# Four of eight contraction tiles of a fused adapter chain computed as a seven-product block scheme, with its first weight streamed from DRAM

## What is computed

```
x = x + (x @ W0.T + b0 + (x @ (2*mask[b]-1)) * coeff[b])   # mask[b]: 1024x1024 int32
x = x + x @ w_eff.T                                        # w_eff: quantised W1 + low rank
x = x + (x @ W2.T + b2 + 2 * (x @ A2[b]) @ B2[b])           # rank 16
x = x + (x @ B3[b].T) @ A3[b].T                            # rank 16
```

## Time and profile before

| | |
|---|---|
| median of 3 runs | 557.78 us |
| the profiled execution's own time | 557.65 us |
| its span, first to last instruction | 555.6 us |
| PE busy | 541.3 us (97%) |
| VectorE (DVE) busy | 398.2 us (72%) |
| ACT busy | 328.9 us (59%) |
| POOL busy | 157.8 us (28%) |
| moved over the span | 80.07 MB, 144 GB/s |

### The profile page before, as it was taken

One profiled execution on the slowest core, in us unless ns is written; L12 is line 12 of the kernel. 1 busy time (PEld: TensorE's weight loads), 2 busy tenths in 40 slices (PEclk: granted clock), 3 DMA queues, 4 the chain that ended last, 5 costly groups with the idle time before them and its releaser, 6 DMA issues.

```text
span 555.6 us, 8876 instructions
## 1 busy us (share of the span) xinstructions
PE 541.3 (97%) x2892; PEld 464.6 (84%) x2892; DVE 398.2 (72%) x622; ACT 328.9 (59%) x622; POOL 157.8 (28%) x170
## 2 busy tenths in 40 slices
PE   5999999999999999999999999999999999999997
PEld 4988888888888788888888888888888888888886
DVE  5998898988956859666765875866687487586631
ACT  3877766776655846564564664656557466564620
POOL 2769778987714040021012002102100300210200
PEclk9999999999999999999999999999999999999999
DMA  8766042733577982574475366256447635634202
GB/s 230 246 88 143 21 145 62 248 97 113 120 192 231 314 204 97 170 186 69 149 221 113 132 187 156 63 170 197 76 151 226 114 119 163 174 73 151 76 0 76
DMA packets 138120, 80.07 MB, mean 144 GB/s; under 512 B 95664, under 2 KB 111024, under 8 KB 138096
## 3 DMA queue, kind: packets, MB, share of 16 engines
q1 hardware_dynamic: 137520, 78.71, 51.8%
q0 software_dynamic: 288, 1.05, 0.5%
q10 hardware_dynamic: 288, 0.01, 0.0%
HBM read 65.59 MB, written 14.16 MB: 144 GB/s over the span
## 4 chain that ended last, share of the span: by engine, by line
PE 84%; DVE 8%; ACT 4%; DMA 3%; issue 1%; POOL 0%; DVEq 0%; ACTq 0%; SPq 0%; POOLq 0%
PE bank L1432 19%; PE bank L1468 10%; PE bank L1469 10%; PE bank L1470 10%; PE bank L1439 10%; PE bank L1306 5%; PE bank L1308 5%; PE bank L1307 5%; PE bank L1478 3%; PE bank L1216 2%; PE bank L1485 1%; DVE merged_ring L1078 1%; DVE w_lo L984 1%; DMA mask_ring<-in_mask_Bx4096x_ik 1%; ACT bank L574 1%; PE bank L1230 1%
## 5 line engine op out<-in xcount | busy, mean ns | idle before, releaser
L1432 PE MATMUL bank<-x_t_pair,m_hi 128*128 128x512 f32 x512 | 128.4, 393 | 1.8 <-ACT m_hi L740 1.6
L740 ACT CAST m_hi<-merged_ring 128x512 fp32r<-128x512 f32 x128 | 73.0, 618 | 66.1 <-PE bank L1439 34.1
L1432 PEld LDWEIGHTS bank<-x_t_pair,m_hi 128*128 128x128 f32 x512 | 92.5, 189 | 19.5 <-ACT m_hi L740 2.6
L1084 DVE TENSOR_TENSOR m_lo<-merged_ring,m_hi 128x512 fp32r<-128x512 f32 x128 | 82.4, 689 | 30.7 <-ACT m_hi L740 30.6
L1468 PE MATMUL bank<-P_hi,x_t_pair 128*128 128x512 f32 x256 | 99.7, 389 | 0.0
L1469 PE MATMUL bank<-P_lo,x_t_pair 128*128 128x512 f32 x256 | 99.7, 389 | 0.0
L1470 PE MATMUL bank<-P_hi,x_t_pair 128*128 128x512 f32 x256 | 99.6, 389 | 0.0
L530 POOL TENSOR_TENSOR x_t_pair<-x_sum,x_t_pair 128x256 fp32r<-128x256 f32 x32 | 24.8, 801 | 260.5 <-ACT x_t_pair L781 260.5
L1078 DVE TENSOR_TENSOR merged_ring<-merged_ring,w_t 128x1024 f32<-128x1024 f32 x64 | 78.3, 1234 | 21.6 <-ACT merged_ring L730 20.6
L730 ACT ACTIVATE merged_ring<-mask_ring,batch_now 128x1024 f32<-128x1024 int32 x64 | 77.9, 1241 | 23.1 <-DMA mask_ring<-in_mask_Bx4096x_ik 22.3
L1439 PEld LDWEIGHTS bank<-x_t_pair,m_lo 128*128 128x128 f32 x512 | 69.9, 190 | 5.0
(11 more groups left out here) (152 smaller groups left out, 869.6 us busy)
## 6 DMA issues: line engine op xcount, KB each, us to landing
mask_ring<-in_mask_Bx4096x_ik SPq DMA_DIRECT2D x64, 512.0 KB, 4.5
out<-out_staged SPq DMA_DIRECT2D x32, 256.0 KB, 2.1
w_nat<-in_L_cond_W SPq DMA_DIRECT2D x14, 512.0 KB, 5.1
x_t_squares<-in_x SPq DMA_DIRECT2D x56, 128.0 KB, 2.7
w_raw<-in_L_cond_weight SPq DMA_DIRECT2D x16, 256.0 KB, 4.5
g_batch<-g_dram SPq DMA_DIRECT2D x32, 128.0 KB, 4.5
w0t_dram<-w_out SPq DMA_DIRECT2D x14, 256.0 KB, 2.7
w_t<-w0t_dram SPq DMA_DIRECT2D x6, 512.0 KB, 5.2
```

The lines of the kernel that those rows point to most:

```text
L740: nc.scalar.copy(Mh[:, n % MR], ring_f[:, k % MR, h * HALF:(h + 1) * HALF]).then_inc(s["h_set"], 1)
L1084: nc.vector.tensor_tensor(Ml[:, n % MR], ring_f[:, k % MR, h * HALF:(h + 1) * HALF], Mh[:, n % MR].bitcast(F32), ALU.subtract).then_inc(s[ ...
L1432: mm(bank[L0_BANK[HT * h + j]][:, :], Mh[:, n % MR, j * P:(j + 1) * P], xThl[:, :, :, k + i, :], start=(k + i == 0), stop=False, skip_grou ...
```

## The change

It treats k-tiles 0 to 3 of main's product as a 2x2 block product: x1's tiles 0 to 3 give blocks of two k-tiles by 128 tokens, P's give blocks of two k-tiles by 512 columns. Instead of eight block products it makes seven in batches 1 to 7 (batch 0 stays as it was, `plain_batch`). The sums of P's blocks (T1 to T4) are made once, by POOL at the end of batch 0, and split into hi and lo by ACT and VectorE in batch 1. The sums of x1's blocks (S1 to S4) are made in every batch: four additions on VectorE (`a_sums`), four roundings on ACT (`a_hi`), four remainders on VectorE (`a_lo`). The products that several outputs share are added up on VectorE (`c11_seen`, `c22_sums`, four additions per batch), the biases of two sums on POOL. k-tiles 4 to 7 are as before. The outputs are now made in the order (0,0), (1,0), (0,1), (1,1) and closed one after another.

T needs the place of the resident `w0t`. So from batch 1 on each part's W0 rows, 512 KB, are loaded from `w0t_dram` into `land`, which has room for two parts (`load_w0`): the load of part j waits for merged(j-2). These eight loads per batch are in the same SP list as the masks. `out_add` of output 2 moves to between m_lo(0) and m_lo(1).

```
-            def batch(b, first=False, last=False):
-                for k in range(MR, KT):
-                    if k == MR + 2 and not first:
-                        store(b - 1, 1)
...
-                    sp.wait_ge(s["m_ready"], 2 * KT * b + 2 * (k - MR) + 2)
-                    load_mask(b, k)
...
+            def load_w0(b, j):
+                sp.wait_ge(s["v_set"], KT * b + j - 1)
+                sp.dma_start(land[:, j % 2].rearrange("p (i n) -> p i n", i=2),
+                             w0t_dram[part_rows(j), :, part_cols(j)].rearrange("k p n -> p k n")).then_inc(w0_land[j % 2], 16)
+            def next_mask(b, k):
+                done = 2 * KT * b + 2 * k + 2
...
+                    sp.wait_ge(s["m_ready"], done)
+                    load_mask(b, k + MR)
...
+                    load_mask(b + 1, k - MR)
...
+            def load_next(b, last):
                 if not last:
+                    for k in range(MR, KT):
+                        next_mask(b, k)
+                        if k < MR + 2:
+                            load_w0(b + 1, k - MR)
                     sp.wait_ge(s["m_used"], 2 * KT * (b + 1))
                     load_x(b + 1)
...
+            def batch(b, last=False):
+                load_w0(b, 2)
+                store(b - 1, 0)
+                load_w0(b, 3)
+                next_mask(b, 0)
+                next_mask(b, 1)
+                load_w0(b, 4)
+                load_w0(b, 5)
+                store(b - 1, 1)
+                load_w0(b, 6)
+                load_w0(b, 7)
+                next_mask(b, 2)
+                next_mask(b, 3)
+                sp.wait_ge(s["out_done"], 4 * b)
+                load_tables(b)
+                load_next(b, last)
...
+            def a_hi(b):
+                act.wait_ge(s["a_summed"], 4 * b)
+                for i in range(4):
+                    nc.scalar.copy(Ph[:, 0:2, a_cols(i)], Ss[:, 0:2, a_cols(i)]).then_inc(s["a_hi"], 1)
...
+            def c11_seen(b):
+                dve.wait_ge(s["prod_done"], 4 * b - 3)
+                nc.vector.tensor_tensor(c_sum[:, :], bank[MAIN_BANK[0]][:, :], b2all[:, 0:HALF], ALU.add).then_inc(s["c11_seen"], 1)
...
+                nc.vector.tensor_tensor(c_sum[:, :], c_sum[:, :], bank[P6_BANK][:, :], ALU.add).then_inc(s["c11_c6"], 1)
...
                     merged(b, 1, first)
-                    for k in range(2):
-                        m_lo(b, k)
+                    m_lo(b, 0)
+                    out_add(b - 1, 2, second)
+                    m_lo(b, 1)
+                    if second:
+                        t_lo(T1)
                     merged(b, 2, first)
                     merged(b, 3, first)
-                    out_add(b - 1, 1, 0)
+                    out_add(b - 1, 3, second)
                     merged(b, MR, first)
-                    out_add(b - 1, 1, 1)
                     merged(b, MR + 1, first)
...
                     if k == MR + 2:
                         merged(b, KT - 1, first)
+                        if not first:
+                            a_sums(b, second)
+                if not first:
+                    a_lo(b)
...
+            def product(o, left, right, start=False, stop=False):
+                (lh, ll), (rh, rl) = left, right
+                mm(o, lh, rh, start=start, stop=False, skip_group_check=True)
+                mm(o, lh, rl, start=False, stop=False, skip_group_check=True)
+                return mm(o, ll, rh, start=False, stop=stop, skip_group_check=True)
...
+            def batch(b):
+                layer0(b)
+                for kk in range(2):
+                    pe.wait_ge(s["x1_ready0"], HT * b + kk + 1)
+                    ins = product(bank[MAIN_BANK[0]][:, :], x1_of(kk, 0), p_of(kk, 0), start=(kk == 0), stop=(kk == 1))
+                ins.then_inc(s["prod_done"], 1)
+                pe.wait_ge(s["t_ready"], 4)
+                for o, i, j in ((P6_BANK, S2, T2), (MAIN_BANK[2], S1, T1), (MAIN_BANK[1], S3, T3)):
+                    pe.wait_ge(s["a_ready"], 4 * b - 3 + i)
...
+                rank(b)
+                pe.wait_ge(s["c11_seen"], b)
+                for kk in range(2):
+                    product(bank[MAIN_BANK[0]][:, :], x1_of(2 + kk, 0), p_of(2 + kk, 0))
+                main(b, 0, range(HT, KT))
+                close(b, 0)
+                pe.wait_ge(s["v1_set"], b)
+                for kk in range(2):
+                    product(bank[MAIN_BANK[1]][:, :], x1_of(2 + kk, 1), t_of(T4, kk))
+                main(b, 1, range(HT, KT))
+                close(b, 1)
+                pe.wait_ge(s["v2_set"], b)
+                pe.wait_ge(s["a_ready"], 4 * b)
+                for kk in range(2):
+                    product(bank[MAIN_BANK[2]][:, :], sum_of(S4, kk), p_of(2 + kk, 1))
+                main(b, 2, range(HT, KT))
+                close(b, 2)
+                main(b, 3, range(HT, KT), True)
+                close(b, 3)
```

More of the change, by code:

```diff
@@ L432, in _ @@
             batch(NB - 1, last=True)
-            store(NB - 1, 1)
+            for pair in range(2):
+                store(NB - 1, pair)
             for h in range(2):
@@ L527, in x1_lo @@
             def x1_lo(b):
+                if not isinstance(b, int):
+                    pool.wait_ge(s["a_summed"], 4 * b)
                 for o in range(HT):
@@ L781, in x1_hi, with batch @@
                 nc.scalar.copy(x1h[:, o], x1s[:, o]).then_inc(s["x1_hi"], 1)
-            def batch(b, first=False, last=False):
+            def batch(b, first=False, last=False, second=False):
                 if not first:
@@ L796, in batch @@
                     m_hi(b, k, first)
+                    if second and k in (MR - 1, MR):
+                        t_hi(T4 if k == MR - 1 else T3)
                     if first and k == MR - 1:
@@ L822, in _ @@
             batch(0, first=True)
-            with act.Fori(1, NB - 1) as b:
+            batch(1, second=True)
+            with act.Fori(2, NB - 1) as b:
                 batch(b)
@@ L1161, in batch @@
                         merged(b, MR, first)
+                    if second and k <= MR:
+                        t_lo((T2, T4, T3)[k - 2])
                     if not first and k == MR:
@@ L1173, in batch @@
                     x1_lo(b, o)
+                if not first:
+                    c11_seen(b)
                 if not last:
@@ L1180, in batch @@
                 nc.vector.tensor_tensor(Us[rows, :], usum[rows, :], Us[rows, :].bitcast(F32), ALU.subtract).then_inc(s["u_ready"], 1)
+                if not first:
+                    dve.wait_ge(s["u_ready"], b + 1)
+                    c22_sums(b)
                 if not last:
@@ L1188, in _ @@
             batch(NB - 1, last=True)
-            for t in range(2):
-                for h in range(2):
-                    out_add(NB - 1, t, h)
+            for i in range(4):
+                out_add(NB - 1, i)
         @block.tensor
@@ L1483, in close @@
                     pe.wait_ge(s["u_ready"], b + 1)
                     pe.wait_ge(s["g_in"], 64 * (b + 1))
-                mm(bank[MAIN_BANK[2 * t + h]][:, :], Us[:, t * P:(t + 1) * P], Gs[:, h * HALF:(h + 1) * HALF], start=False, stop=True).then_inc(s["out_done"], 1)
-            def batch(b, first=False, last=False):
-                layer0(b, first)
-                main(b, 0, 0, range(HT))
-                main(b, 0, 1, range(HT))
-                rank(b)
-                main(b, 0, 0, range(HT, KT))
-                main(b, 0, 1, range(HT, KT))
-                close(b, 0, 0)
-                close(b, 0, 1)
-                for h in range(2):
-                    main(b, 1, h, range(KT))
-                    close(b, 1, h)
@@ L1500, in _, with plain_batch @@
-            batch(0, first=True)
+                mm(bank[MAIN_BANK[i]][:, :], Us[:, t * P:(t + 1) * P], Gs[:, h * HALF:(h + 1) * HALF], start=False, stop=True, skip_group_check=True).then_inc(s["out_done"], 1)
+            def plain_batch():
+                layer0(0, True)
+                for i in range(2):
+                    main(0, i, range(HT), True)
+                rank(0)
+                for i in range(2):
+                    main(0, i, range(HT, KT))
+                for i in range(2):
+                    close(0, i)
+                for i in range(2, 4):
+                    main(0, i, range(KT), True)
+                    close(0, i)
```

195 lines of the change are left out of this document (156 added, 39 removed).

## The result

| | before | after |
|---|---|---|
| median of 4 runs each on one chip, us | 558.31 (557.56 to 559.66) | 601.59 (598.12 to 602.77) |
| ratio, 95% interval | | 1.0762 (1.0712 to 1.0812) |
| profiled execution: own time, span, us | 557.65, 555.6 | 602.77, 601.0 |
| batch 1, us | 46.83 | 61.33 |
| batches 2 to 7, mean, us | 46.83 | 51.78 |

Slower by 7.6%: the side that the prediction held likeliest, but 32.6 us beyond the end of its range. A batch is the distance from one start of layer0 on PE's timeline to the next; after, layer0 starts at 225.67, 287.00, 338.47, 390.50, 442.94, 495.61 and 546.87, and the last close starts at 597.43 (one distance, 0.23 us, ends the last batch). Against compute-bound batches of 45.47 the time goes so: batch 0 is 1.25 us longer, batch 1 loses 15.9, the six others 6.31 each, 37.8. With the 9.5 us saved that is +45.4, and the spans differ by 45.4.

The account below looks back on a forecast made before the run. PE was taken to bound the kernel, busy 97% of the span. From 557.65 us, -9.5 for removed matmuls, + 6 x 2.0 of stalls and + 0.7 for batch 1 gave 560.9, rounded 561.0; range 551.5 to 569.

Parts of the forecast that it names:

- what is removed: PE, batches 1 to 7: 42 matmuls instead of 48 over k-tiles 0 to 3, saving 9.5 us in all.
- the chain of the *moved* steps: Batch starts from batch 2: late third output delays W0(5)'s issue (+1.63), m_lo(2) (2.82 + L), step 7 (L + q + 16.4).
- L: Landing time of W0 part 5's load after issue: taken as 4.8 us, bounds 3.8 and 5.5.
- q: Queueing added to the 3.8 us landing of part 6's mask: taken as 0.3 us, bounds 0 and 1.2.
- The stall by the formula: PE's wait per batch from batch 2, L + q - 3.1: 2.0 us, bounds 0.7 and 3.6.
- the gaps at L1604 and L1611: Sign on PE, batches 2 to 6: gaps before step 2's m_lo matmuls and step 7, about 2 us in all.
- These I put at nothing: POOL's ten block sums, batch 0's main and batch 1's start: 24 to 31 us once, with bias sums costed at nothing.
- Batch 1's extra: Batch 1's own added time, from an earlier chain start with t_lo and t_hi in between: 0.7 us, bounds 0.2 and 1.5.
- VectorE's and ACT's additions: Per batch, VectorE's eight 256-element and four 512-element operations and ACT's four a_hi fit idle time, costing nothing.
- transfers do not queue: Rival on the DMA loads: L = 3.8, q = 0, stall 0.7 us, time 552.5 us; chance 0.25.
- break-even: Rival on the DMA loads: L + q from 4.4 to 4.9, time 556 to 559 us; chance 0.17.
- x comes late too: Rival: next x, loaded after the last mask, lands 4.5 us late, 1 us x 6 more, 567 to 570; chance 0.10.

Follow-up runs that it names:

- everything else off: Changed kernel without W0 loads from batch 2 on, POOL's sums as fills, m_lo(1) before output 2's addition, c_sum's bias on VectorE: 552.88 us, 0.9924 of before.

## Why the prediction was wrong

**Right:** what is removed. 42 matmuls for 48 save 1.36 us a batch: in the changed kernel main takes 23.15 us in the batch from 390.50 (419.79 to 442.94), where it took 24.51, and all that the batches lose is lost in layer0. Right too, and this is the instructive part, is the chain of the *moved* steps: W0(5) issued 1.63 us into layer0 (1.7 measured), m_lo(2) at 2.82 + L (9.82 with the measured 7.0; measured 400.49 - 390.50 = 9.99), step 7 at L + q + 16.4 (26.1; measured 416.72 - 390.50 = 26.22). The stall by the formula, 7.0 + 2.7 - 3.1 = 6.6, against 52.44 - 45.47 = 7.0 measured. With each batch's own two landings the formula gives 5.7, 5.7, 6.6, 6.9, 5.5 and 5.3 for batches 2 to 7; measured are 6.0, 6.6, 7.0, 7.2, 5.8 and 5.3. So ACT idle until mask 6 and the gaps at L1604 and L1611 came as told, and main in the batches has none; only that the second gap shows first before step 5, and not before step 7, was not told.

**Wrong, first: the sizes of L and q** ("Lower bound 3.8, upper 5.5, the longest in these rows"; "0.3, because the issues are some 1.2 to 1.5 us apart"). In the batch from 390.50 L is 7.0 and q 2.7. Over batches 2 to 7 L is 6.2 to 7.0 and q 1.7 to 3.4, outside their bounds in every one; on average 6.6 and 2.5, 4.0 us a batch more than taken. The measured stall is 6.3 where 2.0 was forecast, 26 us over six batches, more than half of what the forecast lacks. The bounds were landings of loads alone or in pairs; the changed kernel issues four loads of 512 KB within 4.2 us (387.99 to 392.2), and two stores right behind. A row on pairs bounds nothing about a queue of four. The trace of the kernel before had longer ones, too: a mask issued behind another mask and four loads of tables landed after 7.2 us in batch 1 and 6.1 in batch 2. My own number said it: one takes 1.6 us to move at 318 to 330 GB/s and the last three are issued 1.0 and 1.1 us apart, so each is later than the one in front, and the engines still had mask 5 to finish. Measured over the window from 393 to 399:

```profile
393.00:399.00 6.00, 5.33 (x28) 4.10 (x26) 1.01 (x1) 3.90 (x6) 0.00 (x0) 1.00 0.85 270
```

270 GB/s, less than the 318 to 330 I reckoned with. The price of the rule of the Trainium skill that I set against it ("DMA: Bandwidth & Descriptors", anatomy of one DMA on its GpSimd path: 2.0 us plus the bytes at 436 GB/s, an estimate of 3.2 us) was further off in a queue: the fastest of the eight landings above is 3.9.

**Wrong, second: "These I put at nothing", of POOL's ten sums.** I gave their length rightly (24 to 31 us; 27.9 measured) and asked only whether POOL had something else due. What they cost is VectorE's time: batch 1 lost 10.2 us by them in the changed kernel, and the kernel before 13.1 in all. Batch 1's extra of 0.7 (bounds 0.2 and 1.5) was 15.9: those 10.2, 4.8 of the stream (56.54 without it), and the rest unassigned. Batch 0's 1.25 belong here as well: without the sums it fell by 1.3, and the sums alone added 1.1.

**Wrong, third, and small:** VectorE's and ACT's additions that were put at nothing. The eight operations of 256 elements were priced at 2.7 us; the four a_lo alone take 3.05, three of them beside POOL's remainders, which no sentence of mine asked about. With everything else off, the batches are still 0.8 us above 45.47.

**Wrong, fourth: "PE's clock row stays 1.00".** It fell, see below; I had said that a lower clock would make me wrong by more.

Of the rivals, *transfers do not queue* and *break-even* fell at once. *x comes late too* named a late transfer, but none of the long waits is for x: the page's longest are for w_landing and mask_ring. The sum of the two parts added alone to the kernel before is 23.6 + 13.1 = 36.7 us, less 9.5 that is 27.2; measured are 43.3. The other 16 arise from both together. The stream costs 5.2 us a batch here and 3.0 there, 13 of the 16. One reason can be read: with the stream alone W0(5) is issued between 1.9 us ahead of layer0's start and the start itself in batches 2 to 7, here 1.7 us behind it, because VectorE comes later to the merged that frees its place. That this is the whole reason is not shown.

## What to carry to other kernels

Count the transfers in flight at the moment a new one is issued, in the changed order: a landing time read from a shorter queue is a lower bound and no range. Bytes in flight counted for much here, but that they alone give the landing was not shown; taking two stores from behind W0(5) brought it only 0.7 us. Before work is put on GpSimd because it is idle there, look at which VectorE operations with both operands in SBUF run beside it: they take turns with it. The same holds the other way round, for work put on VectorE where GpSimd is busy. And when a buffer that was loaded once becomes a stream, price the stream first: 4 MB a batch cost more than the matmuls that its freed room paid for.
